# An adaLN feed-forward kernel on one core: the feed's first block begun inside the attention's last two tiles, its weights split by GpSimd alone

## What is computed

```python
h = shift_token(x)                      # half of the channels from the row above
q, k, v = split(h @ wqkv); q, k = rotary(l2norm(q) * qs, l2norm(k) * ksc)
x = x + local_attention(q, k, v) @ wo   # 8 heads of 64, each row sees itself and the 256 rows before it
h = shift_token(x)
h = (h - mean) / sqrt(var + 1e-5) * lg + lb
a, g = split(h @ w1 + b1)               # 2 x 1365 columns
x = x + (a * gelu(g)) @ w2 + b2
```

## Time and profile before

| | |
|---|---|
| time, median of 3 runs | 3183.95 us (3183.66 to 3187.36) |
| the profiled execution, its own time | 3186.28 us |
| its span, first to last instruction | 3184.1 us |
| mean granted TensorE clock | 0.982 |
| PE busy | 3071.0 us, 96% of the span |
| DVE busy | 1838.7 us, 58% |
| ACT busy | 1484.5 us, 47% |
| POOL busy | 1032.2 us, 32% |

### The profile page before, as it was taken

One profiled execution on the slowest core, in us unless ns is written; L12 is line 12 of the kernel. 1 busy time (PEld: TensorE's weight loads), 2 busy tenths in 40 slices (PEclk: granted clock), 3 DMA queues, 4 the chain that ended last, 5 costly groups with the idle time before them and its releaser, 6 DMA issues.

```text
span 3184.1 us, 48197 instructions
## 1 busy us (share of the span) xinstructions
PE 3071.0 (96%) x16534; PEld 2561.8 (80%) x16534; DVE 1838.7 (58%) x3933; ACT 1484.5 (47%) x3198; POOL 1032.2 (32%) x1671
## 2 busy tenths in 40 slices
PE   9998999999968999999999999999986999999999
PEld 8986888888857788888877888888875788887887
DVE  4655888888864333333324888888875344333432
ACT  2116888888852111111113888888882111111111
POOL 1306666666635000000044566666647000000000
PEclk8999999999989999999999999999997999999999
DMA  4421111222123111100131122111114110111110
GB/s 152 140 78 36 65 60 67 67 67 67 54 77 93 40 40 40 40 8 33 40 121 41 57 68 67 59 65 67 61 59 131 53 36 25 53 47 53 54 40 20
DMA packets 149778, 194.49 MB, mean 61 GB/s; under 512 B 23286, under 2 KB 90998, under 8 KB 149284
## 3 DMA queue, kind: packets, MB, share of 16 engines
q1 hardware_dynamic: 133700, 175.69, 16.8%
q10 hardware_dynamic: 15840, 15.73, 1.5%
HBM read 120.06 MB, written 41.95 MB: 51 GB/s over the span
## 4 chain that ended last, share of the span: by engine, by line
PE 95%; DVE 2%; issue 1%; POOL 1%; ACT 1%; DVEq 0%; SPq 0%; ACTq 0%; POOLq 0%
PE bank L345 25%; PE bank L347 25%; PE bank L346 24%; PE bank L814 6%; PE bank L793 6%; PE bank L776 5%; PE bank L580 3%; PE bank L869 1%; DVE a_PT L1363 0%; PE bank L588 0%; DVE f_h L1481 0%; PE bank L605 0%; ACT a_PT L1074 0%; DVE f_hraw L1489 0%; ACT f_hT_hi L1155 0%
## 5 line engine op out<-in xcount | busy, mean ns | idle before, releaser
L1174 ACT ACTIVATE f_gate<-bank,f_b 128x512 f32<-128x512 f32 (+1 forms) x176 | 121.4, 690 | 997.2 <-PE bank L347 997.1
L345 PE MATMUL bank<-f_hT_hi,f_w_hi 128*128 128x512 f32 (+1 forms) x1408 | 556.5, 395 | 16.3 <-ACT f_hT_hi L1155 15.0
L1517 DVE SCALAR_TENSOR_TENSOR f_uraw<-bank,f_b,f_gate 128x512 f32<-128x512 f32 (+1 forms) x176 | 132.1, 751 | 750.7 <-ACT f_gate L1174 750.5
L347 PE MATMUL bank<-f_hT_hi,f_w_lo 128*128 128x512 f32 (+1 forms) x1408 | 552.9, 393 | 0.0
L346 PE MATMUL bank<-f_hT_lo,f_w_hi 128*128 128x512 f32 (+1 forms) x1408 | 552.0, 392 | 0.0
L345 PEld LDWEIGHTS bank<-f_hT_hi,f_w_hi 128*128 128x128 f32 (+1 forms) x1408 | 260.9, 185 | 78.4 <-ACT f_hT_hi L1155 15.7
L347 PEld LDWEIGHTS bank<-f_hT_hi,f_w_lo 128*128 128x128 f32 (+1 forms) x1408 | 260.6, 185 | 64.2
L346 PEld LDWEIGHTS bank<-f_hT_lo,f_w_hi 128*128 128x128 f32 (+1 forms) x1408 | 261.0, 185 | 62.5
L1069 ACT ACTIVATE a_P<-a_S,a_bias 128x384 f32<-128x384 f32 x512 | 309.4, 611 | 3.9 <-DVE a_bias L1352 3.8
L1352 DVE CUSTOM_DVE_ANT_0 a_S<-bank,a_masks,a_q 128x384 f32<-128x384 f32 x512 | 295.7, 615 | 24.0 <-PE bank L776 18.9
L1062 ACT ACTIVATE a_P<-a_P,a_inv 128x384 f32<-128x384 f32 x512 | 287.3, 613 | 2.1 <-DVE a_inv L1358 0.5
(11 more groups left out here) (166 smaller groups left out, 6559.9 us busy)
## 6 DMA issues: line engine op xcount, KB each, us to landing
a_h<-x_layer_in SPq DMA_DIRECT2D x128, 128.0 KB, 2.8
a_res<-x_layer_in SPq DMA_DIRECT2D x64, 256.0 KB, 2.9
x_after_attention<-out_tiles SPq DMA_DIRECT2D x64, 256.0 KB, 2.0
f_res<-x_after_attention SPq DMA_DIRECT2D x64, 256.0 KB, 3.4
f_stage<-in_L_ffn_w SPq DMA_DIRECT2D x60, 256.0 KB, 3.6
a_V<-a_V SPq DMA_DIRECT2D x28, 512.0 KB, 5.1
f_h<-x_after_attention ACTq DMA_DIRECT2D x28, 512.0 KB, 4.5
c_x<-in_x SPq DMA_DIRECT2D x32, 256.0 KB, 3.1
```

The lines of the kernel that those rows point to most:

```text
L345: pe.matmul(dst, w[0], m[0], start=start, stop=False)
L347: return pe.matmul(dst, w[1], m[0], start=False, stop=stop)
L1517: dve.scalar_tensor_tensor(f_uraw[0:ROWS[m], m % 2, :], bank[pair_of(u, m, end)][0:ROWS[m], :], f_b1[0:ROWS[m], 0, m:m + 1], f_gate[0:ROWS ...
```

## The change

The feed's first block is taken up inside the attention's last steps.

- SP: the load of f_h moves from step 31 to the head of step 30, and behind it go the six loads of the small vectors (f_ln, f_b1) and, as before, the staged weights of m=0 and 1. The weights of m=2 are staged in step 32, once m=0 is split. f_b2 has a semaphore of its own and is loaded behind a_over.
- DVE: normalize(block 0) stands at the end of step 30. raw(0) and raw(1) stand in step 31 behind mask_max(31, 7), lo(0), lo(1), raw(2), raw(3) behind inverse(31, 3), lo(2) and lo(3) behind o_sum(31, 0, 1). The waits for a_over and for the stores go; the latter move to m=7.
- PE: the 16 transposes of block 0 stand in step 31 on both sides of p_T(31, 1) and go to banks 2, 3, 1 and 0, each as its head has been read. feed_up(0), the a half of up(0), stands behind project_out(30), feed_up(1), the g half, behind pv(31, 1), both to banks 2 and 3. project_out(30) waits for raw(3), project_out(31) for result(30).
- ACT: the four hi copies stand in step 31. The hi casts of the weights go.
- POOL: in step 31, behind o_lo(30, 1), it splits up 0, down 0 and up 1; in the feed down 1, which waits for project_out(31), and then m=2 to 10, both hi and lo.

```diff
-        SPLIT_BY_ACT = 3
+        FIRST_TURNS = (bank[2], bank[3], bank[1], bank[0])
...
+        def up_pair_of(blk, u, m, end):
+            return 2 if blk == 0 and m == 0 else pair_of(u, m, end)
...  SP, attention
-                        if t == TILES - 1:
+                        if t == TILES - 2:
                             sp.wait_ge(a_w_lo, START + 4 * (l + 1))
-                            for done in (a_q_mm, a_k_mm, a_v_mm):
+                            for done in (a_hT_mm, a_k_mm):
                                 sp.wait_ge(done, START + (l + 1) * TILES)
                             for i in range(2):
                                 sp.wait_ge(a_stored[i], START + (l * (TILES // 2) + QUAD // 2) * 16)
                             load_shifted_block(sp, x_mid, f_h, row_of(0, 0), f_h_in)
+                            load_feed_vectors()
                             stage_up(sp, l, 0)
                             stage_down(sp, l, 0)
                             stage_up(sp, l, 1)
                             stage_down(sp, l, 1)
+                        if t == TILES:
+                            for done in (f_w1_hi, f_w1_lo, f_w2_hi, f_w2_lo):
+                                sp.wait_ge(done, START + HM * l + 1)
+                            stage_up(sp, l, 2)
+                            stage_down(sp, l, 2)
...  PE, attention
+                    if x == TILES - 2:
+                        pe.wait_ge(f_hT_raw, START + l * FHTS + KT_)
+                    if x == TILES - 1:
+                        pe.wait_ge(a_out_set, START + G + x)
...
+                def feed_h_T(k):
+                    if k == 0:
+                        pe.wait_ge(f_h_normed, START + (l * BLOCKS + 1) * QUAD)
+                    pe.wait_ge(a_S_masked, START + (G + TILES - 1) * H + (5, 6, 8, 7)[k])
+                    block_h_T(k, FIRST_TURNS[k])
+
+                def feed_up(which):
+                    if which == 0:
+                        pe.wait_ge(f_hT_hi, START + l * FHTS + KT_)
+                        pe.wait_ge(f_hT_lo, START + l * FHTS + KT_)
+                    up_half(l, 0, which, up_pair_of(0, 0, 0, False), 0)
...
                         if here(t - 1):
                             pv(t - 1, 1)
+                        if t == TILES:
+                            feed_up(1)
...
+                        if t == TILES - 1:
+                            feed_h_T(0)
+                            feed_h_T(1)
                         if here(t):
                             p_T(t, 1)
+                        if t == TILES - 1:
+                            feed_h_T(2)
+                            feed_h_T(3)
...
                         if here(t - 1):
                             project_out(t - 1)
+                        if t == TILES - 1:
+                            feed_up(0)
...  DVE, attention
+                        if t == TILES - 1:
+                            feed_h_T_raw(0)
+                            feed_h_T_raw(1)
...
                             p_T(t, 1)
                             inverse(t, 3)
+                        if t == TILES - 1:
+                            feed_h_T_lo(0)
+                            feed_h_T_lo(1)
+                            feed_h_T_raw(2)
+                            feed_h_T_raw(3)
...
                             o_sum(t, 0, 1)
+                        if t == TILES - 1:
+                            feed_h_T_lo(2)
+                            feed_h_T_lo(3)
...
                             sums(1, t + 2)
+                        if t == TILES - 2:
+                            normalize(l * BLOCKS)
...  DVE, feed
-                dve.wait_ge(a_over, START + l + 1)
-                normalize(l * BLOCKS)
-                dve.wait_ge(f_small_in, START + (l + 1) * (7 * 16))
-                for i in range(2):
-                    dve.wait_ge(a_stored[i], START + (l + 1) * (TILES // 2 * 16))
-                for k in range(KT_):
-                    h_T_raw(l * FHTS + k, bank[4 + k], k)
-                    h_T_lo(l * FHTS + k, k, 0)
...  POOL, attention
+                    if t == TILES - 1:
+                        pool.wait_ge(a_k_rotated, START + G + TILES)
+                        for done in (a_q_mm, a_k_mm, a_v_mm):
+                            pool.wait_ge(done, START + G + TILES)
+                        split_up(l, 0)
+                        split_down(l, 0)
+                        split_up(l, 1)
...  POOL, feed
+                split_down(l, 1)
+                for m in range(2, HM):
+                    split_up(l, m)
+                    split_down(l, m)
```

More of the change, by code:

```diff
@@ L672, in condition, with block_h_T, up_half @@
                 heads.q()
+            def block_h_T(k, dst):
+                for j in range(QUAD):
+                    mm = pe.transpose(dst[:, j * P:(j + 1) * P], f_h[:, j, k * P:(k + 1) * P], ident[:])
+                mm.then_inc(f_hT_mm, 1)
+            def up_half(l, m, which, base, u):
+                pe.wait_ge(f_w1_hi, START + l * HM + m + 1)
+                pe.wait_ge(f_w1_lo, START + l * HM + m + 1)
+                for k in range(KT_):
+                    mm = three_passes(pe, bank[base + which][0:ROWS[m], :],
+                                      [f_w1[m][i][:, which, k, :] for i in range(2)],
+                                      [f_hT[u][i][:, k, :] for i in range(2)], k == 0, k == KT_ - 1)
+                mm.then_inc((f_a_mm, f_g_mm)[which], 1)
             def attention(l):
@@ L893, in up @@
                             pe.wait_ge(a_q_squared, START + (l + 1) * TILES + 1)
[L894 to L901 removed]
+                        for which in range(2):
+                            up_half(l, m, which, pair_of(u, m, end), u)
                     def next_h_T(k):
@@ L1173, in one_block @@
                         act.wait_ge(f_u_raw, START + (n * HM + m - 1 if m >= 2 else n * HM))
-                        act.activation(f_gate[0:ROWS[m], m % 2, :], bank[pair_of(u, m, end) + 1][0:ROWS[m], :], ACT.Gelu,
+                        act.activation(f_gate[0:ROWS[m], m % 2, :], bank[up_pair_of(blk, u, m, end) + 1][0:ROWS[m], :], ACT.Gelu,
                                        bias=f_b1[0:ROWS[m], 1, m:m + 1]).then_inc(f_gelu, 1)
@@ new lines, in scale, with h_T_raw @@
+            def scale(count):
+                for j in range(QUAD):
+                    dve.tensor_scalar(f_h[:, j, :], f_h[:, j, :], f_mv[:, j, 0:1], f_rs[:, 1, j:j + 1],
+                                      ALU.subtract, ALU.mult).then_inc(f_h_normed, 1)
+            def h_T_raw(count, src, k):
+                dve.wait_ge(f_hT_mm, START + count + 1)
+                if k >= 2:
+                    dve.wait_ge(f_hT_lo, START + count - 1)
+                dve.tensor_scalar(f_hraw[:, k % 2, :], src[:], f_ln[:, 0, k:k + 1], f_ln[:, 1, k:k + 1],
+                                  ALU.mult, ALU.add).then_inc(f_hT_raw, 1)
@@ L1559, in one_block @@
                             after.q()
+                        if m == 7 and blk == 0:
+                            dve.wait_ge(f_b2_in, START + (l + 1) * 16)
+                            for i in range(2):
+                                dve.wait_ge(a_stored[i], START + (l + 1) * (TILES // 2 * 16))
                         if m == 7:
```

214 lines of the change are left out of this document (98 added, 116 removed).

## The result

The changed kernel took 3140.74 us (median of 4 runs, 3139.72 to 3141.36), the kernel before 3185.65 us beside it (4 runs, 3183.66 to 3188.81). The ratio is 0.9857, with a 95% interval of 0.9845 to 0.9869: 44.9 us faster. The forecast of 3130.5 us was 10.2 us too low, the range of 3121 to 3148 held. Of these 10.2 us, 1.7 are the kernel before itself: its median beside the changed kernel was 3185.65 us, and the forecast had subtracted from 3183.95. The rest is gain that didn't come: 53.5 us forecast, 44.9 measured. The profiled execution took 3140.15 us, its span is 3138.0 us, which is 46.1 us under the span of before.

What follows compares the result with a forecast made beforehand. TensorE (PE) bounds the kernel, losing time locally at each layer's passage from attention to feed. Savings of 26.4 and 27.1 us, 53.5 together, off the median of 3183.95 gave 3130.5 us, range 3121 to 3148.

Steps and rivals of the forecast that it cites:

- The norm, 7.8 us quiet: DVE, between inverse(31,1) and result(29): block 0's norm takes 7.8 us with POOL idle, 15.4 at the other end.
- Rival (a): Norm on DVE not quiet: 15.4 instead of 7.8 us, 7.6 more in each passage; 3145.5 us, chance 0.12.
- The idle time of PE ahead of heads 6 and 7: Step 31: PE stands some 5.5 us because result(29), behind the norm, frees bank 0 late.
- The lo passes beside POOL: Tail of attention: DVE's lo passes, stretched while POOL splits weights, add 0.6 us a passage, ends 0 and 2.
- project_out(30): PE in the tail: starts at 931.15 us and keeps its 4.42 us at a mostly low clock.
- The early up-projection: PE in the tail: feed_up(0) takes 2.73 us at full clock; feed_up(1) fills idle time, costing 0 to 0.2 us.
- Rival (c): Early up matmuls at low clock (4.8 us) or m=2 and m=3 late (3 us): 3136 to 3146 us, chance 0.09.
- Block 1's statistics, 0.5 us: Feed's first block: this DVE work now lies fully beside POOL's splits, costing 0.5 us in each layer.
- POOL alone splits: Tail and feed: POOL makes all hi and lo splits without ACT; cost nothing, if late 1 to 3 us a passage.
- (b): Tail runs faster, pv(31,0) and project_out(30) at 2.4 GHz, no lo stretched: 4 us more each, 3122.5 us, chance 0.09.
- (d): Slower than before: PE stays at 1.2 GHz into the feed's first block, up to 3278 us; chance 0.02.
- (e): Early pieces wait for attention's end, up(1) starts where it did; chance 0.02 together with a gain under 0.2%.

Runs made afterwards that it cites:

- e7: Changed kernel with eight more bn_stats (same values again) ahead of block 0's norm on DVE: 3150.97 us, ratio 0.9887.
- e5: Changed kernel with POOL's first weight split of the tail waiting until lo(0) and lo(1) are written: 3139.31 us, ratio 0.9848.
- e10: Changed kernel with ACT again casting the hi halves of m=2's up weights ahead of its first Gelu: 3139.36 us, ratio 0.9850.
- e1: Changed kernel with block 1's bn_stats and aggregation moved to m=1 in the feed's first block, small steps left at m=2: 3134.16 us, ratio 0.9840.
- e3: Changed kernel without early up-projection, and with block 0's transposes, raw, hi and lo back behind attention: 3169.01 us, ratio 0.9949.
- e2: Changed kernel without feed_up(0) and feed_up(1) in attention, up(0) back at the head of the feed: 3144.06 us, ratio 0.9870.
- e9: Changed kernel with the edits of e1 and e5 together: 3132.97 us, ratio 0.9829.

## Why the prediction was right, and where it fell short

- **What bounds the kernel**: right. The waits of 17.1 and 7.50 us were the loss, and taking them out moved everything behind forward.
- **The loads**: neither DVE nor PE waited for f_h, the vectors or the weights; no wait of PE for f_w1 or f_w2 is in the trace of after. The load of m=3 left SP at 951.36 us instead of 948 and was there at 957.7, not by 953. That cost POOL 0.29 us of waiting and PE none, since POOL itself came to m=3 only at 957.5.
- **The norm, 7.8 us quiet** (the step on the earlier trace rows): 7.66 us measured, and e7 shows that more time there is paid in full. Rival (a) fell, for POOL was quiet as read.
- **The idle time of PE ahead of heads 6 and 7, some 5.5 us**: 4.64 and 4.53. Its size doesn't enter the sum, since DVE sets the time there.
- **The lo passes beside POOL, 0.6 us with bounds 0 and 2**: 2.60 us for the first pair, against 1.29 with POOL held back (e5): 1.3 us, twice the value. The total fits all the same, because two errors cancel. The sum took 0.8 us of DVE's waits for PE and ACT off behind result(29), but 5.38 us passed there (918.47 to 923.85), as in the kernel before: the subtraction of p_T(31,0) ended 6.2 us late, not 5.7. From the subtraction of p_T(31,1) to project_out(30), in turn, the tail grew by 0.2 us and not by 0.6, since DVE worked through waits of 1.92 and 1.57 us that it had had there. So project_out(30) came 7.15 us late, where the sum had 6.4 and 0.6.
- **project_out(30), 4.42 us**: 4.42 us in the first layer, but that is luck. The prediction had the low clock of the new gap last to about 935. It didn't: the granted clock is 0.50 in 919.2 to 921.8 us and 1.00 in 925 to 930.5, pv(31,0) takes 1.66 us and not 2.90, and the clock falls once more (0.61 in 933.8 to 938.2) behind the 3.50 us that PE waits for p_T(31,3). In the second layer, behind the same wait, project_out(30) ran at the full clock (last section), which is why that passage gained 28.6. The premise that the first matmuls go at 1.2 GHz after every long idle time wasn't borne out by its own rows either: project_out(31) follows 2.97 us of idle time and its first matmul takes 0.47 us, the next four 0.39 or 0.40.
- **The early up-projection**: 2.74 us for feed_up(0) (938.84 to 941.58), 0.17 us of idle time behind feed_up(1), as said, and 2.84 us for project_out(31), where the sum had 2.7. Rival (c), low clock in the early matmuls, didn't come.
- **The distance from inverse(31,1) to up(1), 36 to 39 us**: 38.14 and 36.95.
- **Block 1's statistics, 0.5 us** (the term of the sum that was mis-sized): 3.4 and 3.6 us. I saw that the chain now lies fully beside POOL's splits and that PE had been idle for 0.77 us there, and priced the overlap at 0.5 us; the chain became 0.99 us longer in the first layer and 2.00 in the second. And I misread the 0.77 us: it said that PE already waited for this chain, so that any delay goes to PE whole, 1.77 us here, and behind the longer gap the clock fell, 1.6 us more. The quiet chain, 5.9 us, stood in the earlier trace rows and the stretched one in the trace of before; the sum gave this term no bounds, and none of the rivals was this one.
- **POOL alone splits, nothing**: 0.2 to 0.5 us a passage for m=2 by e10, nearly nothing. That its splits now run beside DVE's chain is the term above.
- **Rivals (b), (d), (e)**: (b) came in part. pv(31,0) went at the full clock in both layers and project_out(30) in the second, worth 1.2 us there; in the first, DVE worked without a break from 926.80 to 937 us, and the quicker pv(31,0) gave nothing that shows. (d) and (e) didn't come: the low clock behind the new gap was over by 925 us.
- **The rest**: 2.7 us of the profiled run were lost by 299 us, with the clock low in the first attention's fill, which some profiled runs have and others don't. With the term at its true size the sum would have been 47.5 us instead of 53.5: 3136.5 against the median of 3183.95, 3138.2 against the 3185.65 measured beside it. 3140.74 was measured. Another 2.7 us for the clock of the fill would reach that, but whether the median executions have it isn't shown: for those that weren't profiled only the mean clock is known (0.988 to 0.991).

## What to carry to other kernels

When a change pulls work forward, look at the first place behind it where the bounding engine already waits a little. A wait of 0.8 us there meant no slack at all: what the change delayed was paid whole, with the clock on top. A chain of dependent steps on a few elements was stretched to twice its length by the engine beside it, and cutting it in two and starting it earlier (e1) took the wait away. And the round of transpose, raw, hi and lo, worth 25.0 us between e3 and e2, cost little inside waits that another pipeline already had.

## What the runs showed of the hardware

**The clock behind short gaps.** A wait of 2.54 us of PE was followed by 8 matmuls at 1.2 GHz, behind three at 2.4 (granted clock 0.85 and 0.76 in 979 to 988), and the 2.04 us in e10's first layer by as many. One of 0.77 us was followed by none (1.00), and neither were the 1.55 us in e2 and the 1.88 us in e3's second layer. The Trainium skill (TensorE: Matmul & The Clock Gate, section on HAM oscillation) describes how idle gaps between bursts put PE back to half its clock; the trace agrees, in a stretch that was full up to the gap. But the gap alone doesn't decide: behind a wait of 3.50 us project_out(30) had 8 matmuls at the low level in the first layer of after, and in the second, behind 3.49 us, it ran at 1.00:

```profile
2376.00:2380.00 4.00, 3.02 (x17) 2.62 (x18) 3.87 (x6) 0.81 (x1) 2.44 (x2) 1.00 0.00 0
```

So the same instructions gave passages 1.2 us apart in after and 2.7 apart in e9. Together with the 2.7 us of the first attention's fill that makes up to 5.4 us, a part of the scatter between executions, which for the kernel before reached from 3182.69 to 3191.86 us over all its runs.

**DVE beside POOL.** Steps on 128x4 elements took up to 1.23 us instead of 0.16, a pair of lo passes 2.60 instead of 1.29, and four scale passes 4.46 instead of 1.92; four bn_stats took 2.46 and 2.45. For the lo passes an edit shows that POOL is the cause (e5 holds it back and changes nothing else), and no DMA ran beside the stretched pair in after (share 0.00 in 925 to 930.5 us); for the others it is the comparison of stretches with POOL busy and quiet.

```profile
981.51 4.46 DVE L1372 TENSOR_SCALAR f_h<-f_h,f_mv,f_rs 128x512 f32<-128x512 f32 x4
```
